# Two mixture-of-experts stages: lists ordered by choice, results added to rows in memory, weights split on GpSimd

## The reference, cut to what matters

```
logits = xf @ gate_w.T;  probs = softmax(logits)
top_p, top_i = top_k(probs, 2);  w = top_p / (sum(top_p) + 1e-9)
capacity = int(1.25 * T / E)                      # 640 of T = 4096, E = 8
rank = cumsum(one_hot(top_i), axis=0) - 1         # per choice and expert
keep = my_rank < capacity
for e in range(E):
    g = silu(xf @ gate_proj_w[e].T);  u = xf @ up_proj_w[e].T
    out += comb[:, e:e+1] * ((g * u) @ down_proj_w[e].T)
```

## Time and profile before

| | us |
|---|---|
| runs: median, lowest, highest of 3 | 1774.78, 1768.44, 1775.36 |
| profiled execution: its own time | 1769.27 |
| profiled execution: span of the core, first to last instruction | 1767.2 |
| TensorE / VectorE / ScalarE / GpSimd busy in it | 1212.8 / 1021.9 / 629.5 / 510.0 |
| granted TensorE clock, mean | 0.814 |

### The profile page before, as it was taken

One profiled execution on the slowest core, in us unless ns is written; L12 is line 12 of the kernel. 1 busy time (PEld: TensorE's weight loads), 2 busy tenths in 40 slices (PEclk: granted clock), 3 DMA queues, 4 the chain that ended last, 5 costly groups with the idle time before them and its releaser, 6 DMA issues. The chain is left out here.

```text
span 1767.2 us, 26688 instructions
## 1 busy us (share of the span) xinstructions
PE 1212.8 (69%) x9140; PEld 801.2 (45%) x9214; DVE 1021.9 (58%) x2340; ACT 629.5 (36%) x989; POOL 510.0 (29%) x571
## 2 busy tenths in 40 slices
PE   4625977959635059704888998899889997412991
PEld 2413856839524059702343443344434443311991
DVE  5855555655426136446777776777777770630662
ACT  4632221222111023201265664665566665001330
POOL 2434013040026747712003000300120000374772
PEclk9666988969755579955699998999999998555995
DMA  1439611020120133160000010001000100213325
GB/s 45 155 145 390 266 37 59 0 95 0 36 63 28 53 106 99 52 185 6 7 19 7 10 46 8 7 7 43 8 7 8 31 7 13 62 53 90 98 68 162
DMA packets 109057, 114.06 MB, mean 65 GB/s; under 512 B 8720, under 2 KB 90512, under 8 KB 108048
## 3 DMA queue, kind: packets, MB, share of 16 engines
q1 hardware_dynamic: 96608, 91.98, 16.5%
q0 software_dynamic: 9216, 19.02, 3.2%
q10 hardware_dynamic: 3120, 1.57, 0.3%
HBM read 49.34 MB, written 59.02 MB: 61 GB/s over the span
## 5 line engine op out<-in xcount | busy, mean ns | idle before, releaser
L1829 DVE TENSOR_REDUCE att_mx<-att_ps 128x1 f32<-128x512 f32 (+3 forms) x768 | 405.2, 555 | 146.9 <-PE att_ps L1722 111.3
L1603 ACT ACTIVATE att_prob<-att_ps 128x1024 f32<-128x1024 f32 (+3 forms) x384 | 300.3, 812 | 228.9 <-PE att_ps L1734 176.7
L1719 PE MATMUL att_ps<-att_kT,att_q1T 128*128 128x512 bf16 (+3 forms) x709 | 235.1, 344 | 50.5 <-DVE att_mx L1829 34.2
L1731 PE MATMUL att_ps<-att_q2T,att_kT 128*128 128x512 bf16 (+3 forms) x753 | 201.1, 331 | 3.2 <-ACT att_prob L1603 1.2
L1719 PEld LDWEIGHTS att_ps<-att_kT,att_q1T 128*128 128x128 bf16 x768 | 74.2, 98 | 259.1 <-DVE att_mx L1829 211.7
L978 POOL DMA_INDIRECT sides<-moe_ys,moe_back_i x160 | 153.2, 958 | 87.6 <-issue 47.3
L1745 PE MATMUL att_pso<-att_prob,att_v 128*32 128x512 f32 (+3 forms) x1536 | 163.9, 499 | 1.6
L972 POOL DMA_INDIRECT slots<-moe_rows,moe_place_i x128 | 123.2, 963 | 59.4 <-issue 38.4
L1499 POOL CAST att_qm_rows<-att_nm 128x32 bf16<-128x32 f32 x48 | 15.6, 324 | 395.8 <-DVE att_nm L1838 391.6
L1722 PE MATMUL att_ps<-att_mask,att_identb 128*128 128x128 bf16 x512 | 115.8, 228 | 2.3 <-DVE att_mx L1829 1.5
L1071 PE MATMUL moe_ps_t<-moe_ident,moe_xs 128*128 128x128 f32 x160 | 27.0, 290 | 115.2 <-DMA moe_xs<-slots 115.2
(11 more groups left out here) (283 smaller groups left out, 2439.5 us busy)
## 6 DMA issues: line engine op xcount, KB each, us to landing
slots<-fw_zeros SPq DMA_DIRECT2D x2, 5200.0 KB, 30.1
moe_xs<-slots SPq DMA_DIRECT2D x16, 650.0 KB, 4.9
sides<-fw_zeros SPq DMA_DIRECT2D x2, 4096.0 KB, 35.3
moe_side<-sides SPq DMA_DIRECT2D x16, 512.0 KB, 6.2
tok<-prep_tok SPq DMA_DIRECT2D x4, 1536.0 KB, 5.4
turned<-prep_tT SPq DMA_DIRECT2D x4, 1536.0 KB, 8.7
fw_tok<-tok SPq DMA_DIRECT2D x4, 1536.0 KB, 10.4
fw_Tkv<-turned SPq DMA_DIRECT2D x4, 1024.0 KB, 6.7
```

What stands on the lines that cost most here:

```text
L1603: nc.scalar.activation(prob[(2 * n + pair) % 4][:, :, 0:size], ps2[pair][:, :, 0:size], ACT.Exp, scale=SCORE_SCALE).then_inc(exp_done, 1)
L1719: last = nc.tensor.matmul(out[:, 0:size], q1T[t % 2][:, j * P:(j + 1) * P], kT[t][h][:, 512 * c:512 * c + size], start=True, stop=not diag ...
L1731: last = nc.tensor.matmul(ps2[pair][:, h, 0:size], kT[t][2 * pair + h][:, i * P:(i + 1) * P], q2T[t % 2][:, first:first + size], start=Tru ...
L1829: nc.vector.reduce_max(mx[:, c, j, h:h + 1], ps1[(n * QUAD + h) % 2][:, 0:size], AX.X).then_inc(max_done, 1)
```

## The change

- The lists are ordered by choice: first the first-choice lists of the eight experts, then the second-choice lists. 16 lists of 640 rows are worked in two blocks each (3 and 2 tiles), 32 blocks.
- All 32 first-choice scatters come before the 32 second-choice ones, with a semaphore for each half, so that loads of the first lists (325 KB each, a ring of six buffers) wait for the first half alone.
- Results are returned by an indirect transfer that adds to the tokens' rows in memory (`compute_op=ALU.add`). Before the first return of a second-choice list GpSimd waits until all returns of first-choice lists have landed. `sides`, its loads, the additions and the store are gone; the second stage copies the rows to the output with four transfers from memory to memory. The token tensors get 10240 spare rows for empty list entries, which are cleared.
- Weighing moves from VectorE to ScalarE, one instruction per tile, into one buffer per expert that both its lists use.
- The split of the weights, both parts, goes to GpSimd at the end of the fast-weight stage.
- Statistics of the first quarter come before the waits for constants, and its normalization right behind.

```diff
@@ fast_weight_stage, GpSimd, after its loop over chunks
+            pool.wait_ge(expert["loaded"], 3 * 16)
+            for whole, (hi, lo) in expert["split"]:
+                for e in range(EXPERTS):
+                    nc.gpsimd.tensor_copy(hi[:, e], whole[:, e])
+                pool.drain()
+                for e in range(EXPERTS):
+                    nc.gpsimd.tensor_tensor(lo[:, e], whole[:, e], hi[:, e].bitcast(F32), ALU.subtract)
...
@@ expert_stage
+BLOCKS = ((0, 3), (3, LIST_TILES))
-    BLOCKS = [(0, 4), (4, 8), (8, EXPERT_TILES)]
-    blocks = EXPERTS * PER
+    blocks = LISTS * PER
+    RING = 6
...
@@ SyncE
-            sp.wait_ge(slots_written, TILE_COUNT * 2 * 16)
-            for e in range(EXPERTS):
-                if e >= 3:
-                    sp.wait_ge(t_psum, (e - 2) * PER)
-                    sp.wait_ge(back_done, e - 2)
-                sp.dma_start(xs[e % 3][:], slots[e * 2 * CAPACITY:(e + 1) * 2 * CAPACITY].rearrange("(j p) n -> p j n", p=P)).then_inc(xs_loaded[e % 3], 16)
...
+            for i in range(LISTS):
+                if i % EXPERTS == 0:
+                    sp.wait_ge(slots_written[i // EXPERTS], TILE_COUNT * 16)
+                if i >= RING:
+                    sp.wait_ge(t_psum, (i - RING + 1) * PER)
+                    sp.wait_ge(y_done, (i - RING + 1) * PER)
+                    sp.wait_ge(back_done, i - RING + 1)
+                sp.dma_start(xs[i % RING][:], slots[i * CAPACITY:(i + 1) * CAPACITY].rearrange("(j p) n -> p j n", p=P)).then_inc(xs_loaded[i % RING], 16)
+
+            if x_out is not None:
+                for e in range(EXPERTS):
+                    sp.wait_ge(added[e], 2 * LIST_TILES * 16)
+                for b in range(BATCH):
+                    sp.dma_start(x_out[b], x[b * SEQ:(b + 1) * SEQ]).then_inc(stored, 16)
...
@@ GpSimd
-            for b in range(quarters):
-                pool.wait_ge(placed, b + 1)
-                for j in range(tiles):
-                    for k in range(2):
+            for k in range(2):
+                for b in range(quarters):
+                    if k == 0:
+                        pool.wait_ge(placed, b + 1)
+                    for j in range(tiles):
...
-            for n in range(blocks):
-                e, (first, end) = n // PER, BLOCKS[n % PER]
-                pool.wait_ge(y_done, n + 1)
-                for j in range(first, end):
-                    pool.indirect_dma_start(sides, bass.IndirectOffsetOnAxis(ap=back_i[e % 2][:, j:j + 1], axis=0), ys[n % 4][:, j - first], None).then_inc(y_written[n % 4], 16)
+            for i in range(LISTS):
+                k, e = i // EXPERTS, i % EXPERTS
+                if i == EXPERTS:
+                    for first in range(EXPERTS):
+                        pool.wait_ge(added[first], LIST_TILES * 16)
+                pool.wait_ge(back_done, i + 1)
+                for n, (first, end) in enumerate(BLOCKS):
+                    pool.wait_ge(y_done, i * PER + n + 1)
+                    for j in range(first, end):
+                        pool.indirect_dma_start(x, bass.IndirectOffsetOnAxis(ap=back_i[:, i, j:j + 1], axis=0), ys[e][:, j], None, compute_op=ALU.add).then_inc(added[e], 16)
+            for e in range(EXPERTS):
+                pool.wait_ge(added[e], 2 * LIST_TILES * 16)
...
@@ ScalarE, after the second SiLU of a block, for the block before
+            def weigh(n):
+                i, (first, end) = n // PER, BLOCKS[n % PER]
+                k, e = i // EXPERTS, i % EXPERTS
+                act.wait_ge(y_psum, n + 1)
+                if k and first == 0:
+                    act.wait_ge(added[e], LIST_TILES * 16)
+                for j in range(first, end):
+                    share = xs[i % RING][:, j, D + 1:D + 2] if k == 0 else xs[i % RING][:, j, 0:1]
+                    last = nc.scalar.activation(ys[e][:, j], ps_y[n % 2][:, j - first], ACT.Copy, scale=share)
+                last.then_inc(y_done, 1)
...
@@ VectorE, head
+            statistics(0)
+            dve.wait_ge(iotas, 4)
...
-            dve.wait_ge(weights_in, 4 * 16)
             dve.wait_ge(setup, SETUP)
-            statistics(0)
+            normalize(0)
             statistics(1)
-            normalize(0)
             statistics(2)
             statistics(3)
+            dve.wait_ge(weights_in, 4 * 16)
...
@@ VectorE, tail
-            for b in range(quarters):
-                dve.wait_ge(side_loaded[b % 2], (b // 2 + 1) * 32)
-                mine = x[:, b * tiles:(b + 1) * tiles]
-                nc.vector.tensor_tensor(side[b % 2][0][:], side[b % 2][0][:], side[b % 2][1][:], ALU.add)
-                dve.drain()
-                nc.vector.tensor_tensor(mine, mine, side[b % 2][0][:], ALU.add).then_inc(summed, 1)
```

More of the change, by code:

```diff
@@ L874, in expert_stage @@
         hid = [[sb(f"hid{s}{k}", [P, 512]) for k in range(2)] for s in range(2)]
-        ys = [sb(f"ys{s}", [P, 4, D]) for s in range(4)]
-        side = [[sb(f"side{s}{k}", [P, tiles, D]) for k in range(2)] for s in range(2)]
+        ys = [sb(f"ys{e}", [P, LIST_TILES, D]) for e in range(EXPERTS)]
         ps_t = [ps(f"ps_t{s}", [P, 512]) for s in range(2)]
@@ L982, in _ @@
             act.wait_ge(weights_in, 4 * 16)
-            nc.scalar.activation(tri[:], tri_f[:], ACT.Copy).then_inc(setup, 1)
-            if split_weights:
-                act.wait_ge(weights["loaded"], 3 * 16)
-                for e in range(EXPERTS):
-                    nc.scalar.activation(wg_hi[:, e], wg[:, e], ACT.Copy).then_inc(parts_hi, 1)
-                    nc.scalar.activation(wu_hi[:, e], wu[:, e], ACT.Copy).then_inc(parts_hi, 1)
+            nc.scalar.activation(tri[:], tri_f[:], ACT.Copy).then_inc(tri_cast, 1)
             def copy_xt(b):
@@ L1004, in hi @@
             def hi(n):
-                size = P * (BLOCKS[n % PER][1] - BLOCKS[n % PER][0])
+                first, end = BLOCKS[n % PER]
+                size = P * (end - first)
                 act.wait_ge(t_psum, n + 1)
@@ L1020, in _ @@
                         hi(n + 1)
+                if n >= 1:
+                    weigh(n - 1)
+            weigh(blocks - 1)
         @block.tensor
@@ L1045, in ranks @@
                 pe.wait_ge(chosen_done, b + 1)
+                pe.wait_ge(tri_cast, 1)
                 if b >= 2:
@@ L1074, in gate_up @@
             def gate_up(n, k):
-                e, (first, end) = n // PER, BLOCKS[n % PER]
+                e, (first, end) = n // PER % EXPERTS, BLOCKS[n % PER]
                 size, half = P * (end - first), slice(k * P, (k + 1) * P)
@@ L1099, in _ @@
             pe.wait_ge(ranks_read, quarters)
-            if split_weights:
-                pe.wait_ge(weights["loaded"], 3 * 16)
             turn(0)
@@ L1232, in returns @@
                 dve.drain()
-                for k in range(2):
-                    nc.vector.scalar_tensor_tensor(back[:, k], number[k], float(k * TOKENS - 1), empty[:, k], ALU.add, ALU.add)
+                nc.vector.scalar_tensor_tensor(empty[:], number, 0.0, spare_token[:, i], ALU.is_equal, ALU.mult)
                 dve.drain()
-                if e >= 2:
-                    for s in range(4):
-                        uses = [n for n in range(s, (e - 1) * PER, 4)]
-                        dve.wait_ge(y_written[s], 16 * sum(BLOCKS[n % PER][1] - BLOCKS[n % PER][0] for n in uses))
@@ L1257, in _ @@
             for n in range(blocks):
-                e, size = n // PER, P * (BLOCKS[n % PER][1] - BLOCKS[n % PER][0])
+                first, end = BLOCKS[n % PER]
+                size = P * (end - first)
                 for k in range(2):
```

132 lines of the change are left out of this document (43 added, 89 removed).

## The result

| kernel, median us | runs | us | ratio to before |
|---|---|---|---|
| before | 4 | 1773.86 | |
| changed | 4 | 1798.44 (1796.11 to 1800.98) | 1.0153 [1.0135, 1.0171] |

The change costs 24.6 us: 1798.4 was measured where 1700 was forecast. The profiled execution of the changed kernel is one of the four (1800.98; span 1799.2), so its span lies 32.0 above that of before (1767.2), 7 more than the medians say.

A forecast was written before the change was run, and what follows sets the result against it. GpSimd's issue of 144 indirect transfers per stage, 1.262 us apart, was taken as the bound. Savings of 43.5 and 31.1 us, together 74.6, took 1769.3 to 1694.7; 5.5 for the median gave 1700, range 1688 to 1790.

The forecast's parts named there:

- The price of an adding return: GpSimd's issue of 160 returns: bounds 0.958 and 1.92 us each, taken as 0.96, no dearer than a plain one.
- break-even: GpSimd's returns: 0.47 us more per return (74.6 / 160) would use up the whole forecast gain.
- issue much dearer, slower than before: Rival, chance 0.18: GpSimd's adding returns cost up to double, 153 us more, 1853 in all.
- head: Stage start to first scatter: earlier first-quarter statistics and the split moved away save 4.9 us, then 1.4 in the second stage.
- pauses among scatters: First-choice scatters: GpSimd idles 2.3 and 1.9 us for the next quarter's places, +4.2 us per stage.
- gap: GpSimd idle between scatters and returns: early list loads remove it whole, −19.2 and −20.3 us.
- wait in the middle: Before the ninth list GpSimd waits for first-choice adds to land: +2.5 us per stage, bounds 1 and 5.
- tail: After the last return: side loads, additions and store go; 29.2 to 3.1 us (−26.1), second stage 29.1 to 13.0 (−16.1).
- What was costed at nothing: Weighing on ScalarE, smaller blocks, split and clearing: claimed hidden behind GpSimd's returns or other stages' idle time, 0 us.
- a return takes 1.4 or more: Sign in the profile, at GpSimd's returns, that the forecast is wrong; 0.96 us was expected.
- waits for ScalarE: Sign that the forecast is wrong: GpSimd's returns show waits for ScalarE's results.
- that wait for list 8: ScalarE's wait for list 0's adds before weighing list 8: adds land by 639, TensorE arrives at 648 at the earliest.

The follow-up runs named there:

- e1: Changed kernel with its returns as plain scatters (compute_op=add left out, additions lost from the result): 1703.1 us, ratio 0.9619 to before.
- e12: Changed kernel with plain returns into two cleared side tensors, loaded back and added on VectorE, no middle wait: 1708.9 us, ratio 0.9648 to before.
- e13: Same kernel as e12, but lists loaded only when all scatters have landed: 1743.0 us, ratio 0.9839 to before.
- e5: Changed kernel with the last wait of both stages moved from GpSimd to SyncE, second kind of chip: 1822.5 us, ratio 0.9867 to before.
- e2: Kernel of before with its returns into the side tensors made adding ones: 1868.5 us, ratio 1.0546 to before.
- e7: Kernel of before with only the weight split moved to GpSimd, end of fast-weight stage, second kind of chip: 1844.0 us, ratio 0.9962.

## Why the prediction was wrong

The failed step is one term: **"The price of an adding return ... I take 0.96"**. It measured 1.56. The change was on the losing side of the break-even, 0.60 against the 0.47 that was worked out. The step chose the lower end because scatters and returns of different sizes and targets cost the same; but both of those are plain, so they could say nothing of an add. What came is the rival "issue much dearer, slower than before" (0.18), which begins at +0.4 and was priced at +0.96. One of its arguments, that the issue is work per row, did not hold: three quarters of the extra stand at 32 rows already. The bounds were 0.96 and 1.92 with nothing between them, and the break-even of 1.43 lay half way, so by the rows at hand slower deserved odds nearer to even than 0.20.

The other terms, by the profiled executions:

| term, first / second stage | forecast | measured |
|---|---|---|
| head (start to first scatter) | −4.9 / −1.4 | −5.7 / −2.4 |
| pauses among scatters | +4.2 / +4.2 | +3.3 / +3.2 |
| gap | −19.2 / −20.3 | −18.9 / −20.0 |
| wait in the middle | +2.5 / +2.5 | +2.3 / +2.3 |
| tail | −26.1 / −16.1 | −19.4 / −17.4 |
| sum | −43.5 / −31.1 | −38.4 / −34.3 |

Together −72.7 against −74.6, so the structure was read rightly, though the sum owes its closeness in part to luck: the first tail, 6.7 too short in the forecast, is offset by the heads, the pauses and the second tail, each 1 us or so better than forecast. With 160 × 0.604 = 96.6 the two stages come to +23.9, and the medians say +24.6. The rest of the profiled difference, 5.15 in the fast-weight stage and 2.75 in the attention, is not the change's as far as these runs tell: e1 starts its stage at 511.6, and attention took 722.9 before, 725.7 after, 724.7 in e1, 721.6 in e12 and 726.5 in e13.

One size besides was off: the **tail of the first stage**, 3.1 forecast and 9.8 measured. It was taken from how fast the next stage followed SyncE's last store, in a kernel whose GpSimd had been done for 29 us. Once GpSimd is the last to finish, nearly 8 us of its own come last (e5). The second tail, where SyncE's copy runs besides, was 13.0 forecast and 11.7 measured.

What was costed at nothing stayed hidden on this chip: weighing on ScalarE (0.37 us each, 0.38 the bound), smaller blocks, the split, the clearing. Of the signs named in advance, "a return takes 1.4 or more" is the one that came; the returns showed no waits for ScalarE beyond the 0.30, and the middle pause was 2.3 net. ScalarE did wait, 4.7 us before it weighed the last list (its idle time before 709.89), for returns to leave the buffers that it reuses. The forecast had looked at that wait for list 8 alone; it cost nothing, because GpSimd was behind.

## What to carry to other kernels

Before work is moved into a transfer, ask who issues the transfer: here additions that VectorE did in 9.8 us of a stage's tail became 48 us a stage on the one engine that was already the bound. When the sum hangs on a price that no row has, and its break-even (0.47 us) lies inside its bounds, measure that instruction alone in the old kernel first: e2 adds one argument to a call and answers within its interval of 8 us (that it hit the expected sum to 0.2 is luck). And take the parts of a change apart: three of them were good (the order 34 us by e13, the split 3 to 11 by e7 on the other kind of chip, the head 2.4 in the second stage, by the trace alone), and with before's returns they give 1710 us, 3.5 per cent under before.

## What the hardware showed that was not expected

- An indirect transfer's issue on GpSimd is mostly fixed: 863 ns at 32 rows and 958 at 128 plain, 1315 and 1562 adding; 64 columns cost what 128 do. At 128 rows an add puts 144 packets on the queue where a copy puts 32 (worked out from the totals).
- An adding return lands 3.3 us after its issue began (median of 80, the row below), a plain one 2.2: about 1.7 and 1.2 after the issue ended.
- Where GpSimd was the last to finish, a stage ended 7.9 us after its last indirect transfer even if it waited for nothing (e5), and 9.8 (adding) to 11.7 us (plain) if it waited for the landing.
- Two kinds of chip (or of conditions), 4 per cent apart on the kernel of before, on which this change has opposite signs: 1.0153 and 0.9893.

```profile
x<-moe_ys,moe_back_i POOLq DMA_INDIRECT x80, 3.3
```
